# A fused feature network: the last product's first summand and bias are put into PSUM ahead of the last pass, and the small head matmuls stand behind the last product

## What is computed

```python
w = jnp.einsum('bpf,mf->bpm', features, W_ft) + b_ft        # 1024 x 2 x 5128 by 512 x 5128
accumulator = stm * w
l1_x = jnp.clip(accumulator, 0.0, 1.0).reshape(features.shape[0], -1)
l2_x = jnp.clip(l1_x @ W1.T + b1, 0.0, 1.0)                 # W1 is 32 x 1024
return l2_x @ W2.T + b2                                     # W2 is 1 x 32
```

## Time and profile before

| | |
|---|---|
| median of 3 runs | 406.46 us (406.12 to 406.95) |
| profiled execution, its own time | 406.2 us |
| its span, first to last instruction | 404.4 us |
| granted TensorE clock over it | 1.000 |
| TensorE, VectorE, ScalarE busy | 397.4, 349.9, 193.4 us |

### The profile page before, as it was taken

The page is one execution under the profiler, slowest core; times in us unless marked ns, Lnnn a source line. Parts: engine busy times, 40 slices in busy tenths (PEclk is TensorE's granted clock), DMA queues, the critical chain, the costliest instruction groups (busy, mean ns, idle before and its releaser), DMA issues.

```text
span 404.4 us, 4671 instructions
## 1 busy us (share of the span) xinstructions
PE 397.4 (98%) x1770; PEld 322.7 (80%) x1770; DVE 349.9 (87%) x343; ACT 193.4 (48%) x194; POOL 12.8 (3%) x32
## 2 busy tenths in 40 slices
PE   8989999999999999999999999999999999999995
PEld 6868888888888888888888888888888888888851
DVE  3999999999999999999995799998888755996335
ACT  5456655744485444444443844444444467444200
POOL 1000037000000000000000000000000000000000
PEclk9999999999999999999999999999999999999999
DMA  8999989987776766777416799866677786870000
GB/s 271 396 398 399 319 265 214 371 281 272 254 248 229 230 240 234 255 261 245 146 56 237 267 361 353 334 240 238 234 256 241 220 254 195 255 232 34 2 0 1
DMA packets 30326, 96.39 MB, mean 238 GB/s; under 512 B 3768, under 2 KB 9920, under 8 KB 25056
## 3 DMA queue, kind: packets, MB, share of 16 engines
q1 hardware_dynamic: 29392, 95.18, 68.1%
q0 software_dynamic: 624, 0.66, 0.9%
q10 hardware_dynamic: 288, 0.26, 0.2%
HBM read 96.08 MB, written 0.00 MB: 238 GB/s over the span
## 4 chain that ended last, share of the span: by engine, by line
PE 92%; DVE 3%; DMA 2%; ACT 1%; issue 1%; SPq 0%; DVEq 0%
PE sums L551 89%; DMA open_x<-x_p 2%; DVE xs L422 1%; ACT x_hi L318 1%; PE sums L613 1%; PE sums L657 1%; DVE x_lo_home L399 1%; DVE ws L412 0%; DVE c_early L532 0%; DVE c_early L536 0%; ACT x_hi L307 0%; PE sums L697 0%; DVE c_early L540 0%; PE sums L665 0%; PE sums L671 0%
## 5 line engine op out<-in xcount | busy, mean ns | idle before, releaser
L551 PE MATMUL sums<-x_hi,w_hi 128*128 128x512 f32 x560 | 172.3, 391 | 1.1 <-ACT x_hi L318 1.1
L551 PE MATMUL sums<-x_hi,w_lo 128*128 128x512 f32 x560 | 171.1, 389 | 0.0
L551 PEld LDWEIGHTS sums<-x_hi,w_hi 128*128 128x128 f32 x560 | 105.1, 188 | 25.1 <-ACT x_hi L318 1.9
L551 PEld LDWEIGHTS sums<-x_hi,w_lo 128*128 128x128 f32 x560 | 105.1, 188 | 21.9
L551 PE MATMUL sums<-x_lo_home,w_hi 128*128 128x512 f32 x384 | 117.6, 389 | 0.0
L332 ACT ACTIVATE x_hi<-xs 128x2048 fp32r<-128x2048 f32 x58 | 110.7, 1909 | 5.0 <-DVE xs L439 3.2
L327 ACT ACTIVATE w_hi<-ws 128x512 fp32r<-128x512 f32 x58 | 36.8, 635 | 151.0 <-PE sums L551 148.4
L448 DVE TENSOR_TENSOR x_lo_home<-xs,x_hi 128x2048 fp32r<-128x2048 f32 x40 | 91.5, 2286 | 6.8 <-ACT x_hi L332 6.8
L551 PEld LDWEIGHTS sums<-x_lo_home,w_hi 128*128 128x128 f32 x384 | 72.1, 188 | 15.0
L445 DVE TENSOR_TENSOR w_lo<-ws,w_hi 128x512 fp32r<-128x512 f32 x58 | 39.8, 686 | 11.2 <-ACT w_hi L327 11.0
L432 DVE TENSOR_TENSOR xs<-xs 128x2048 f32<-128x2048 f32 x20 | 45.7, 2283 | 0.0
(11 more groups left out here) (74 smaller groups left out, 171.3 us busy)
## 6 DMA issues: line engine op xcount, KB each, us to landing
xs<-x_p SPq DMA_DIRECT2D x40, 1024.0 KB, 5.6
xs<-x_p SPq DMA_DIRECT2D x56, 512.0 KB, 7.1
ws<-w_p SPq DMA_DIRECT2D x56, 256.0 KB, 3.4
ws<-w_p SPq DMA_DIRECT2D x44, 128.0 KB, 5.0
open_x<-x_p SPq DMA_DIRECT2D x3, 512.0 KB, 6.3
stm_all<-stm SPq DMA_DIRECT2D x1, 1024.0 KB, 7.3
open_x<-x_p SPq DMA_DIRECT2D x2, 256.0 KB, 4.3
open_w<-w_p ACTq DMA_DIRECT2D x2, 128.0 KB, 4.0
```

What stands on the lines that cost most here:

```text
L551: return nc.tensor.matmul(sums[:, bank, :], w[:, m * P:(m + 1) * P], x[:, c * BANK:(c + 1) * BANK], start=start, stop=stop, skip_group_che ...
```

## The change

- A new semaphore `seeded`. At the turn to the last pass ScalarE writes P1 + bias from `c_all[0]` into each of banks 0 to 3 once it has been drained, and the last pass's products all add to what is there: none of them has the start flag. TensorE waits for `seeded` where it waited for `drained`.
- VectorE has two instructions for each bank of block 0 in place of three: times stm, from PSUM, and clip.
- No small matmul stands inside `closing()`. Behind it stand `add_halves(0, 1)`, `add_halves(1, 0)`, the first layer of banks 0, 1, 2 and 3, `second_layer(0, 1)` and `second_layer(1, 0)`.
- The first layer of block 0 is no longer one matmul of 512 columns for each bank with a fold behind it, but four of 128 columns, each in one of the four parts of the array, which add straight to the folded sum in bank 7. So `part` of half 0 holds block 2's share alone and is made right behind `first_layer`.

```diff
+            def seed(b):
+                sc.wait_ge(drained, 16 + b + 1)
+                nc.scalar.activation(sums[:, b, :], c_all[0][:, b * BANK:(b + 1) * BANK], ACT.Identity,
+                                     bias=b_ft_col[:, b // 2:b // 2 + 1]).then_inc(seeded, 1)
...
+                        if 1 <= b <= 4:
+                            seed(b - 1)
...
-                nc.vector.scalar_tensor_tensor(out=c_all[0][:, cols], in0=sums[:, b, :],
-                                               scalar=b_ft_col[:, b // 2:b // 2 + 1], in1=c_all[0][:, cols],
-                                               op0=ALU.add, op1=ALU.add).then_inc(last_sum, 1)
-                dve.wait_ge(last_sum, 2 * b + 1)
-                nc.vector.tensor_tensor(c_all[0][:, cols], c_all[0][:, cols],
-                                        stm_all[:, 0, (b % 2) * BANK:(b % 2 + 1) * BANK], ALU.mult)\
-                    .then_inc(last_sum, 1)
-                dve.wait_ge(last_sum, 2 * b + 2)
+                nc.vector.scalar_tensor_tensor(out=c_all[0][:, cols], in0=sums[:, b, :], scalar=1.0,
+                                               in1=stm_all[:, 0, (b % 2) * BANK:(b % 2 + 1) * BANK],
+                                               op0=ALU.mult, op1=ALU.mult).then_inc(last_sum, 1)
+                dve.wait_ge(last_sum, b + 1)
...
-                if b == 1:
-                    hidden(0, 1)
+            hidden(0, 1)
+            hidden(1, 0)
             result(0, 1)
-            hidden(1, 0)
             result(1, 0)
...
-                    start = first and (f == 0 or f == PASSES or (f == 1 and bank == 4))
+                    start = first and (f == 0 or (f == 1 and bank == 4))
...
+                                if f < PASSES:
+                                    pe.wait_ge(drained, 8 * (f - 1) + b + 1)
+                                else:
+                                    pe.wait_ge(seeded, b + 1)
...
-                        if b == 0:
-                            add_halves(0, 1)
-                        if b == 2:
-                            second_layer(0, 1)
+                add_halves(0, 1, True)
+                add_halves(1, 0, False)
+                for b in range(3):
+                    first_layer_of_bank(b)
+                first_layer_of_bank(3).then_inc(l1_summed, 1)
+                second_layer(0, 1)
+                second_layer(1, 0)
...
+            def first_layer_of_bank(b):
+                m, c = divmod(b, PERSP)
+                pe.wait_ge(act_ready, 3 + b + 1)
+                for q in range(Q):
+                    mm = nc.tensor.matmul(sums[q * L1:(q + 1) * L1, 7, 0:QB], w1_sb[:, c * UT + m, :],
+                                          c_all[0][:, b * BANK + q * QB:b * BANK + (q + 1) * QB],
+                                          start=False, stop=b == 3, skip_group_check=True)
+                return mm
...
-            first_layer(1, 0, 2, 1, True, False)
+            first_layer(1, 0, 2, 1, True, True).then_inc(l1_full, 1)
```

More of the change, by code:

```diff
@@ L141, in feature_net @@
         drained = sem("drained")
+        seeded = sem("seeded")
         idle_zeroed = sem("idle_zeroed")
@@ L607, in step @@
                             if first:
-                                pe.wait_ge(drained, 8 * (f - 1) + b + 1)
+                                if f < PASSES:
+                                    pe.wait_ge(drained, 8 * (f - 1) + b + 1)
+                                else:
+                                    pe.wait_ge(seeded, b + 1)
                             product(b, wh, xh, m, c, start)
@@ L660, in first_layer, with add_halves @@
                 return mm
-            def add_halves(n, h):
+            def first_layer_of_bank(b):
[6 more added lines that the diff above has]
+                return mm
+            def add_halves(n, h, whole):
                 pe.wait_ge(part_ready, n + 1)
@@ L665, in add_halves @@
                     mm = nc.tensor.matmul(sums[q * L1:(q + 1) * L1, 6 + n, 0:QB], add_up[:, :],
-                                          part[:, h, q * QB:(q + 1) * QB], start=True, stop=True)
-                mm.then_inc(l1_summed, 1)
+                                          part[:, h, q * QB:(q + 1) * QB], start=True, stop=whole,
+                                          skip_group_check=True)
+                if whole:
+                    mm.then_inc(l1_summed, 1)
             def second_layer(n, h):
```

## The result

The changed kernel takes 402.04 us (median of 4 runs, 401.62 to 402.61), the kernel before 406.56 us beside it (4 runs, 406.12 to 406.95). The ratio is 0.989, with a 95% interval of 0.9875 to 0.9905: 1.1% faster, 3.9 to 5.1 us. The forecast was 402.1 with a range of 401.6 to 403.1.

A forecast was written before the change was run, and what follows sets the result against it. TensorE, busy 397.4 of 404.4 us, was taken as the bound, with the chain behind its last product. Savings of 1.78 and 2.55 us, 4.33 together, from the median 406.46 gave 402.1 us, range 401.6 to 403.1.

The forecast's parts named there:

- Part 1, `closing()`: TensorE in `closing()`: moving the small matmuls out removes breaks of 0.56 and 1.22 us, 1.78 us less.
- Part 2, the chain: From the last product's start to the last store's issue: 5.95 us becomes 3.40, 2.55 us less.
- Its terms 1.78 and 0.72: 1.78 us: small matmuls leaving `closing()`; 0.72 us: VectorE's L536 dropped from bank 3's chain behind the last product.
- Part 3, the cover: Behind the last product: twenty matmuls, ten passes at 0.13 us, hidden under 1.37 us of waiting; cost 0.
- the two bounds: Small-matmul pass distance: 0.12 to 0.15 us from the fold, 0.11 from a quarter of the 512-column distance.
- The first rival: Small matmuls behind the last product: load and columns add up, ten passes take 2.2 us, 0.83 us return: 402.9; chance 8%.
- Part 4, the seeds: At the turn to the last pass: four more ScalarE writes to PSUM, hidden with 1.0 us to spare; cost 0.
- The rival, that the second store starts only when the first is through: At the kernel's end: the two close stores get in each other's way, 1.0 us comes back: 403.1; chance 7%.
- the 1.6 which the prediction named as a sign of being wrong: At the end: wrong if the span ends more than 1.6 us behind the last store's issue.
- The sum: Whole kernel: 1.78 + 2.55 = 4.33 us less, giving 402.1 us against the median, 1.1% less.
- The parts take turns: Small matmuls behind the last product: four array parts not working side by side, 8.7 us more, 410.8; chance 2%.

The follow-up runs named there:

- order alone: Kernel before with only the fold and `second_layer` of half 1 moved behind the last product: 405.63 us, ratio 0.9979.
- the one without seeds: Changed kernel without ScalarE's early writes into the banks; start flags, waits and three VectorE instructions a bank as before: 403.84 us, ratio 0.9932.
- seeds alone: Kernel before plus ScalarE's early writes of P1 + bias into the banks and two VectorE instructions a bank, nothing moved: 405.0 us, ratio 0.9962.
- ten more passes: Changed kernel with five extra groups of four 128-column matmuls between the folds and bank 0's group, into unread bank 4: 403.19 us, ratio 0.9921.

## Why the prediction was right, point by point

- *Part 1, `closing()`.* Forecast 1.78 us less; the traces have 8.09 and 6.27, 1.82. That the order alone takes the stalls away is shown by the kernel with order alone and by the one without seeds, each of which has 6.27 too. "On the path wholly, since TensorE is the bound there" holds only with the seeds: without them 0.77 us come back behind the last product.
- *Part 2, the chain.* Forecast 3.40 us from last product to last store; 3.44. Two small terms were off and nearly met, which is luck: the first VectorE instruction is 0.06 us shorter, and the store comes 0.11 later. The parts: L536's 0.72 and the 0.06 are the seeds (5.95 to 5.16 with seeds alone, 0.79); the new form of the first layer is 1.71, where I had 1.83 less nothing for the stores.
- *What the prediction had wrong without harm to its sum.* Its terms 1.78 and 0.72 read as the worth of the order and of the seeds. The sum, 2.50, is right (2.55 timed, 2.62 in the traces), the shares are not: order alone gives 0.9 us, seeds alone 1.5. The prediction worked out that VectorE keeps up with two instructions a bank (1.2 us against 1.6) and did not draw the consequence for three (1.85 against 1.6).
- *Part 3, the cover.* Taken as 0.13 us a pass; it is 0.109, so 0.20 us of cover remain where I expected nearly none. Of the two bounds, a quarter of the 512-column distance (0.43 us, so 0.107) was the better one; the fold's own 0.12 to 0.15 held the start of a stream, whose first distance is 0.13 in this trace too. The first rival (load and columns add up) is excluded: TensorE waits for the clip, and ten more passes cost 0.84 and not 1.9 us. The rule of the Trainium skill on row groups ("TensorE: Matmul & The Clock Gate", Part 3, "The mechanism"), that a weight load overlaps with matmuls in flight only when its row group differs, does not hold for these parts side by side: loads of 110 ns and columns worth 107 ns make passes 109 ns apart, where they would be 217 apart if they added up. The same section also lets a load run ahead when it goes to the background weight buffer. The traces fit that, without showing the buffer: each pass's loads start about 2 ns behind the matmuls of the pass before.
- *Part 4, the seeds.* Forecast hidden, with 1.0 us to spare; the fourth is done at 338.33 and wanted at 339.24, 0.9. Twice the work made TensorE wait, so the margin is real and about that wide. ScalarE's rounding for step 62 came 1.5 us later (339.96 less the run's own 0.6, against 337.84), forecast 1.35, and no wait of TensorE followed.
- *The stores.* The rival, that the second store starts only when the first is through (1.0 us), is excluded. But the forecast of no cost at all is off too: it took SyncE's queue to be free 0.47 us behind the first store, as between two loads, and the two stores are issued 0.71 us apart, so the last came 0.11 us late. From the last issue to the end of the span pass 1.66 us against 1.57 before. That is over the 1.6 which the prediction named as a sign of being wrong, and its sum had nothing for it: 0.1 us.
- *The sum.* From step 60 on the traces differ by 1.82 + 2.51 less this 0.10, 4.2 us, where 4.33 was forecast. That the timed medians differ by 4.5 and so meet 402.1 to within 0.1 us says less than it seems: the interval of that difference is 3.9 to 5.1.
- *The parts take turns*: excluded by the same rows; the forty matmul records ahead of bank 3's group, ten passes of four, were through in 1.3 us.

## What to carry to other kernels

A right sum does not show that its terms belong to the edits they are written beside. Before you say what one of two edits is worth, ask what the engines do with that edit alone: here the unbroken TensorE alone met a VectorE that needs 1.85 us a bank against 1.6, and the faster VectorE alone already took 0.72 us off a stall of TensorE. A constant or bias that is known early can be added while an engine has time, in the accumulator itself, so that it costs nothing in the chain behind the last product; here the writes had 0.9 us to spare, and twice as many made TensorE 2.15 us late. And small matmuls that fold or finish earlier results are best put where TensorE waits for somebody anyway, behind the last product, as long as their passes fit under that wait.

## What the runs showed of the hardware

Matmuls of 128 columns with 32 columns of weights, in four parts of the array side by side, all with 128 rows, keep 0.109 us a pass over long streams (ten, then twenty passes), with a weight load of 0.11 us for each part and pass: the loads do not add to the columns. Whether the loads (0.110) or the columns (0.107) set the pace is not shown. A ScalarE write to PSUM of 128x512 takes 0.69 to 0.70 us, as the read of a drain does, and the next instruction starts 0.61 or 0.62 behind it (0.57 or 0.58 behind a drain). A VectorE instruction of 128x512 that reads PSUM and one SBUF operand takes 0.69 us with its scalar as a constant, 0.75 with the scalar from SBUF. Two stores of 2 KB are issued on SyncE's queue 0.71 us apart, 0.68 with ten more passes, when the second waits for the queue; two loads in the earlier trace rows were 0.47 apart.
